# A sandwich of attention and experts: the last residual adds move from GpSimd to VectorE, and VectorE sums seven tiles instead of five

## What is computed

```python
x = x + _layernorm(attention(_layernorm(x)))   # 16 heads of 32, causal, rotary
xt = _layernorm(x)
for e in range(64):                            # 8 of 64 experts for each row
    routed += comb[:, e] * (silu(xt @ Wg[e].T) * (xt @ Wu[e].T) @ Wd[e].T)
shared = sigmoid(xt @ Wse.T) * (silu(xt @ Wsg.T) * (xt @ Wsu.T) @ Wsd.T)
x = x + _layernorm(routed + shared)
```

## Time and profile before

| | |
|---|---|
| median of three runs | 1199.74 us (1198.04, 1199.74, 1199.86) |
| profiled execution, its own time | 1199.09 us |
| its span, first to last instruction | 1197.2 us |
| mean granted TensorE clock | 0.968 of full |
| busy: PE, DVE, ACT, POOL | 91%, 58%, 40%, 52% of the span |
| the end of the kernel, from the issue of the first load of partial sums | 1141.57 us to 1197.2 us |

### The profile page before, as it was taken

The page is one execution under the profiler, slowest core; times in us unless marked ns, Lnnn a source line. Parts: engine busy times, 40 slices in busy tenths (PEclk is TensorE's granted clock), DMA queues, the critical chain, the costliest instruction groups (busy, mean ns, idle before and its releaser), DMA issues.

```text
span 1197.2 us, 24385 instructions
## 1 busy us (share of the span) xinstructions
PE 1085.3 (91%) x6309; PEld 728.9 (61%) x6310; DVE 692.3 (58%) x2354; ACT 473.2 (40%) x1366; POOL 621.0 (52%) x629
## 2 busy tenths in 40 slices
PE   5799899989999989979869999999999999999964
PEld 3455566555566545555537777777777776767721
DVE  3766566556666668857855454444444444444447
ACT  1566567656666642242202222222222222222213
POOL 4333333333333312200127888888888777778824
PEclk9899999999999999979969999999999999999987
DMA  9600000000000051100157999999999989997796
GB/s 350 241 2 1 4 1 2 2 4 2 1 2 1 2 227 55 62 16 12 60 163 173 223 218 248 244 226 235 258 231 255 242 213 269 259 227 160 113 318 251
DMA packets 65713, 166.81 MB, mean 139 GB/s; under 512 B 15314, under 2 KB 16594, under 8 KB 65504
## 3 DMA queue, kind: packets, MB, share of 16 engines
q0 software_dynamic: 38496, 83.95, 31.8%
q1 hardware_dynamic: 27136, 81.88, 19.4%
HBM read 119.85 MB, written 62.65 MB: 152 GB/s over the span
## 4 chain that ended last, share of the span: by engine, by line
PE 68%; DMA 16%; DVE 9%; issue 3%; ACT 2%; POOL 1%; DVEq 0%; POOLq 0%; ACTq 0%
PE ps L906 14%; PE ps L658 14%; DMA sum_rows<-x_t,idx 9%; PE ps L917 7%; PE ps L717 6%; DMA x_t<-x_rows,idx 5%; PE ps L773 4%; PE ps L687 4%; PE ps L890 4%; PE ps L737 4%; PE ps L672 2%; PE ps L809 2%; PE ps L789 1%; PE ps L825 1%; DVE high L1196 1%
## 5 line engine op out<-in xcount | busy, mean ns | idle before, releaser
L906 PE MATMUL ps<-big,work 128*128 x1264 | 300.5, 381 | 0.0
L430 POOL DMA_INDIRECT sum_rows<-x_t,idx x157 | 249.9, 1591 | 56.4 <-issue 37.4
L906 PEld LDWEIGHTS ps<-big,work 128*128 128x128 f32 x1264 | 229.0, 191 | 24.9
L424 POOL DMA_INDIRECT x_t<-x_rows,idx x159 | 165.9, 1043 | 69.9 <-issue 28.3
L658 PE MATMUL ps<-big 128*128 128x384 f32 x512 | 179.1, 493 | 1.5 <-ACT big L501 1.1
L369 POOL TENSOR_TENSOR work<-qkv_all,rope_sb 128x256 f32<-128x256 f32 x64 | 46.6, 728 | 249.4 <-ACT qkv_all L506 249.3
L612 ACT ACTIVATE work<-ps 128x512 f32<-128x512 f32 x159 | 94.9, 597 | 202.7 <-PE ps L890 200.4
L917 PE MATMUL ps<-big,work 128*128 x314 | 160.7, 593 | 0.3 <-issue 0.3
L890 PEld LDWEIGHTS ps<-ident_sb,x_t 128*128 128x128 f32 x636 | 78.1, 142 | 108.6 <-issue 68.3
L998 DVE CUSTOM_DVE_ANT_0 ps<-ps,mask_sb 128x128 f32<-128x128 f32 (+3 forms) x256 | 120.8, 513 | 24.0 <-PE ps L687 23.4
L523 ACT ACTIVATE work<-ps,neg_max 128x128 f32<-128x128 f32 (+3 forms) x256 | 132.4, 528 | 4.3 <-DVE neg_max L998 3.2
(11 more groups left out here) (176 smaller groups left out, 1455.9 us busy)
## 6 DMA issues: line engine op xcount, KB each, us to landing
big<-experts SPq DMA_DIRECT2D x65, 768.0 KB, 7.3
sum_rows<-x_t POOLq DMA_DIRECT2D x4, 2048.0 KB, 10.6
big<-sum_rows SPq DMA_DIRECT2D x8, 768.0 KB, 10.9
x_sb<-x SPq DMA_DIRECT2D x4, 1024.0 KB, 15.5
x_rows<-work SPq DMA_DIRECT2D x16, 256.0 KB, 2.0
sum_rows<-attn_t POOLq DMA_DIRECT2D x2, 2048.0 KB
out<-x_sb SPq DMA_DIRECT2D x16, 256.0 KB, 5.9
x_t<-sum_rows SPq DMA_DIRECT2D x4, 768.0 KB, 13.5
```

Source lines behind the costliest of these rows:

```text
L424: pool.indirect_dma_start(rows[:, q, :], None, x2_rows, bass.IndirectOffsetOnAxis(ap=idx[:, q, 0:1], axis=0), bounds_check=last_row, oob_i ...
L430: pool.indirect_dma_start(all_sums, bass.IndirectOffsetOnAxis(ap=idx[:, q, 1:2], axis=0), y_sb[:, q, :], None, bounds_check=last_sum, oob_ ...
L906: mm = pe.matmul(ps[:, 2 + p, 0:GATEUP], rows_t[:, p, c, :], w_ring[:, slot, c * GATEUP:(c + 1) * GATEUP], start=(c == 0), stop=(c == DC - 1))
```

## The change

GpSimd does no arithmetic at the end. All residual adds are VectorE's, in the turns: turn i, which now runs to 18, ends with the add of tile i-3, so the turns 16, 17 and 18 have little else. SUM_ON_PE now leaves out seven tiles, 0, 3, 5, 8, 10, 13 and 15, which VectorE sums. All outputs wait on one semaphore, s_fin. The loads, ScalarE's work and everything ahead of the end stay as they are, but for line numbers, which are some 10 lower in the changed file.

```diff
--- before.py
+++ after.py
@@ -49,10 +49,8 @@
 FIRST_STEPS = [("xt", 0), ("xt", 1), ("proj", 0), ("xt", 2), ("proj", 1), ("xt", 3), ("proj", 2), ("qkt", 0),
                ("proj", 3), ("qkt", 1)]
 
-LAST_ON_DVE = (TILES - 3, TILES - 1)
 NOWHERE = TABLES * B * S
-SUM_ON_PE = tuple(i for i in range(TILES) if i % 3 != 2)
-LAST_ON_POOL = tuple(i for i in range(TILES) if i not in LAST_ON_DVE)
+SUM_ON_PE = tuple(i for i in range(TILES) if i not in (0, 3, 5, 8, 10, 13, 15))
 
 NORM_X_AT = (BLOCKS - 6, BLOCKS - 5, BLOCKS - 3, BLOCKS - 2)
 
@@ -266,7 +264,6 @@
         s_lnd = sem("s_lnd")
         s_norm = sem("s_norm")
         s_fin = sem("s_fin")
-        s_fin_dve = sem("s_fin_dve")
         s_out = sem("s_out")
         s_x2d = [sem(f"s_x2d{p}") for p in range(2)]
         s_combd = sem("s_combd")
@@ -347,10 +344,7 @@
             for i in range(TILES):
                 sp.dma_start(sums_of(i), all_sums_v[:, i, :, :]).then_inc(s_sums[i], 16)
             for i in range(TILES):
-                if i in LAST_ON_POOL:
-                    sp.wait_ge(s_fin, LAST_ON_POOL.index(i) + 1)
-                else:
-                    sp.wait_ge(s_fin_dve, LAST_ON_DVE.index(i) + 1)
+                sp.wait_ge(s_fin, i + 1)
                 sp.dma_start(out_v[:, i, :], x_sb[:, i, :]).then_inc(s_out, 16)
             sp.wait_ge(s_out, 16 * TILES)
 
@@ -480,11 +474,6 @@
                 pool.wait_ge(s_scatter[p], (full * 2 + (5 if p == 0 else 4)) * 16)
                 pool.sem_inc(s_issue, 1)
             pool.sem_inc(s_routed, 1)
-
-            for i in LAST_ON_POOL:
-                pool.wait_ge(s_norm, i + 1)
-                pool.tensor_tensor(out=x_sb[:, i, :], in0=x_sb[:, i, :], in1=sums_of(i)[:, 0, :],
-                                   op=ALU.add).then_inc(s_fin, 1)
 
         @block.scalar
         def _(act):
@@ -1272,21 +1261,21 @@
                 step(dve.tensor_tensor(out=y, in0=y, in1=sums_of(i)[:, 2, :], op=ALU.add))
                 return y
 
-            for i in range(TILES + 1):
+            for i in range(TILES + 3):
                 if i < TILES:
                     step(dve.bn_stats(stats[:, i, :], total_of(i)))
                     dve.bn_aggr(moments[:, i, :], stats[:, i, :]).then_inc(s_lnb, 1)
-                if i >= 1:
+                if 1 <= i <= TILES:
                     k = i - 1
                     dve.wait_ge(s_lnf, k + 1)
                     step(dve.reciprocal(rstd[:, k:k + 1], rstd[:, k:k + 1]))
                     dve.scalar_tensor_tensor(out=moments[:, k, 0:1], in0=moments[:, k, 0:1], scalar=-1.0,
                                              in1=rstd[:, k:k + 1], op0=ALU.mult, op1=ALU.mult).then_inc(s_lnd, 1)
-
-            for i in LAST_ON_DVE:
-                dve.wait_ge(s_norm, i + 1)
-                dve.tensor_tensor(out=x_sb[:, i, :], in0=x_sb[:, i, :], in1=sums_of(i)[:, 0, :],
-                                  op=ALU.add).then_inc(s_fin_dve, 1)
+                if i >= 3:
+                    k = i - 3
+                    dve.wait_ge(s_norm, k + 1)
+                    dve.tensor_tensor(out=x_sb[:, k, :], in0=x_sb[:, k, :], in1=sums_of(k)[:, 0, :],
+                                      op=ALU.add).then_inc(s_fin, 1)
 
 
 def _constants():
```

## The result

The changed kernel takes 1193.48 us as the median of six runs (1192.49 to 1195.55), against 1198.89 us of the kernel before (six runs, 1196.67 to 1200.60). The ratio is 0.9958, with a 95% interval of 0.9945 to 0.9972: 5.4 us or 0.42% faster.

The account below looks back on a forecast made before the run. VectorE, held up by GpSimd's adds, was taken to bound the tail. +2.11 - 1.07 + 1.44 + 7.80 - 12.56 - 0.24 - 0.47 = -2.99 us, from 1199.74 to 1196.8 us; range 1195.2 to 1199.2.

Parts of the forecast that it names:

- Start: VectorE's saturated stretch begins with tile 2 at 1155.91, in place of tile 1 at 1153.80: +2.11 us.
- Adds at 0.60 us: Thirteen residual adds inside VectorE's turns cost 0.60 us each, start to start: +7.80 us.
- rival (b): VectorE's residual adds do not overlap and cost 0.72 us each: +1.8 us, 1198.6 us; chance 0.12.
- rival (e): VectorE waits each turn for ScalarE's root behind a scaling; at 0.1 us a turn, 1198.2 us; chance 0.07.
- Locked-out time: VectorE's two-input instructions in the tail no longer wait for GpSimd's adds: -8.12 and -4.44 us, together 12.56.
- part 1: GpSimd's arithmetic leaves the tail: VectorE regains 12.56 us, and the adds' going gives nothing more by itself.
- rival (c): Loads, not GpSimd, lengthen VectorE's two-input instructions: over 1220 us; shares a chance of 0.06 with other slower cases.
- TensorE in time: In the tail, TensorE at 2.57 us a tile for nine tiles stays ahead; VectorE stays the bound from tile 2.
- rival (d): TensorE's clock falls in the tail, 5.14 us a tile: about 1208 us; shares 0.06 with other slower cases.
- The stretch: From the first load's issue to the last residual add's end, the terms sum to -2.99 us.
- The end: Behind the last residual add, the last output's transfer and program end take 4.81 us as before.
- Rival (a): TensorE's clock rises at 1150.77 as before: 1195.5 us, chance 0.17; or comes later: up to 1199.3 us, chance 0.06.

Follow-up runs that it names:

- e_one_late: Changed kernel with each residual add one turn late, not three; 1210.63 us, one run.
- e_tiny_last: Changed kernel plus a one-column GpSimd write behind the last tile's scaling; median 1194.00 us, 0.9967 of the kernel before.
- e_tiny_early: Changed kernel plus a one-column GpSimd write behind tile 9's scaling, not the last tile's; median 1194.07 us, 0.9964 of the kernel before.
- e_four_sums: Changed kernel with VectorE summing four tiles (2, 5, 9, 13) and TensorE twelve; median 1188.12 us, 0.9924 of the kernel before.
- e_four_last: Kernel before with the residual adds of tiles 12 to 15 on VectorE, not 13 and 15 alone; median 1195.48 us, 0.9983 of the kernel before.
- e_gp_writes: Changed kernel plus twelve GpSimd memsets of a scratch buffer, behind the scalings of tiles 0 to 11; 1198.11 us, one run.
- e_gp_reads: Changed kernel plus twelve GpSimd adds of two SBUF scratch buffers, behind the scalings of tiles 0 to 11; 1201.92 us, one run.
- e_five_sums: Changed kernel with SUM_ON_PE as before: VectorE sums tiles 2, 5, 8, 11, 14, TensorE eleven; median 1188.95 us, 0.9923 of the kernel before.
- e_warm_four: Changed kernel with VectorE summing tiles 2, 5, 9, 13 and eleven idle TensorE products ahead of the loads; median 1187.88 us, 0.9915 of the kernel before.

## Why the prediction was off

Its steps one by one, in times behind the issue of the first load:

- **Start.** Tile 1 was to land at 6.53 (1148.1 less 1141.57), measured 6.42; tile 2 was to be ready at 14.34, measured 14.13. TensorE's first tile took 5.13 us, 5.24 had been taken. Right.
- **Adds at 0.60 us.** 1160.91 to 1161.51, start to start; rival (b) falls.
- **No wait for ScalarE.** None in the waits; rival (e) falls, and e_one_late shows what it would have cost.
- **Locked-out time.** Every VectorE instruction is at its short length; part 1 holds, and rival (c) falls.
- **TensorE in time.** VectorE never waits behind 1157.33, and TensorE's tiles stay at 2.7 to 2.8 us (six passes, 1177.72 for 2.84): the clock did not fall, and rival (d) falls.
- **The stretch.** The sum made it 47.83 (50.82 - 2.99), measured 47.72. That it fits to 0.1 us is partly luck: the same stretch was 47.19 in e_tiny_last and 48.26 in e_tiny_early.
- **The end.** "The last output then follows as before, 4.81 us." This is the step that failed. I had put down what lies behind the last add as one block, "the last output's transfer and the end of the program", and carried it over. It held two things side by side: the last output's transfer, over 2.4 us behind the add (1192.39 to 1194.8), and GpSimd's closing DRAIN, which ends 5.1 to 5.2 us behind GpSimd's last instruction and set the end. The change takes the second away, and 2.13 us with it. This also answers part 1's sentence that the going of GpSimd's adds "gives nothing more by itself": it gave these 2.13 us. It was to be read: SyncE's last wait of 2.4 us stands in the waits of the profile of before, only under the name of an engine that had long been done.

With that term the forecast would have been -5.1 us, 1194.6 from the median of three runs. Its base was itself 0.85 us high: the same kernel has 1198.89 over six runs. The difference of -5.1 stands against -5.4 measured.

Rival (a), the clock, is left as an uncertainty of size, not of sign. From TensorE's first product to its first finished tile it took 5.24 us before and 5.13 after, but 4.28 us in e_four_sums, 4.30 in e_four_last (1141.75 to 1146.05) and 5.52 in e_gp_writes (1151.48 to 1157.00). The granted clock says the same: it reads 0.50 up to 1154.0 in the changed kernel, 4.4 us behind TensorE's start, and 0.91 on average in the microsecond behind that; in e_four_sums 0.50 up to 1144.0, 2.5 us behind the start, and 0.80 in the next. The rise is not at a fixed delay behind the start of the work, and this is worth 1.2 us from one execution to another; why it came where it did was not settled.

## What to carry to other kernels

Ask of every engine when its last instruction ends, and what the end of the program does to it: an engine that finishes beside the critical path can still own the last microseconds, and moving its last small instruction forward or elsewhere is then worth more than the instruction. When an engine is taken off a stretch, cost its removal twice, once for what it blocks while it works and once for what its absence lets end sooner. And test the parts of a change apart: in the profiles here one part gained 7.9 us and the other gave 2.6 of it back, though on the kernel before that other part cost nothing (-0.6 us). What a part costs depends on what the other has already freed.

## What the runs showed of the hardware

- GpSimd's closing DRAIN took 5.134 us with nothing in front of it in this kernel (changed kernel, e_gp_reads, e_five_sums and others), and 5.26 us from the start of a 0.10 us write (e_tiny_last, e_tiny_early). ScalarE's and VectorE's ended with their last instruction (1190.2 + 1.04 and 1191.2 + 1.24 in the kernel before). Whether GpSimd's is so long only behind indirect DMAs, which all kernels here have, was not tried.
- Two-input VectorE instructions in SBUF were held up by a GpSimd add of 1.27 us by up to 1.1 us (the 0.16 us bias step took 1.26), and not at all by a GpSimd memset of 0.95 us over twice the size.
- Eleven products of 0.87 us each (9.60 us together), thrown away while TensorE waited for a load, went with a stretch 2.3 us shorter (45.44 against 47.72). Where a later load bound VectorE (e_warm_four) no gain from them is shown.
